# A decoder layer with 32 experts on one core: weights stored with index 4p+k instead of 128k+p

## The reference

```
h = rmsnorm(layernorm(x)) * norm_w                    # 1600 rows of 512
logits = h @ router_w.T ; top 4 of 32 experts per row, weights by softmax
gu = h_row @ w1[e]          # 512 x 512 : gate 256, up 256
ys = (silu(g) * u) @ w2[e]  # 256 x 512
out = x + sum over the 4 experts of weight * ys + (silu(h @ sg) * (h @ su)) @ sd
```

## Time and profile before

| what | value |
|---|---|
| median of 3 runs | 1313.39 us |
| the three runs | 1310.71, 1313.39, 1321.99 us |
| profiled execution | 1321.14 us, its span 1319.4 us |
| PE / PEld busy | 1189.7 / 933.1 us |
| DVE / ACT / POOL busy | 808.2 / 592.3 / 351.8 us |
| mean granted PE clock | 0.939 |

### The profile page before, as it was taken

The page is one execution under the profiler, slowest core; times in us unless marked ns, Lnnn a source line. Parts: engine busy times, 40 slices in busy tenths (PEclk is TensorE's granted clock), DMA queues, the critical chain, the costliest instruction groups (busy, mean ns, idle before and its releaser), DMA issues. The chain is left out here.

```text
span 1319.4 us, 20922 instructions
## 1 busy us (share of the span) xinstructions
PE 1189.7 (90%) x7761; PEld 933.1 (71%) x7762; DVE 808.2 (61%) x1392; ACT 592.3 (45%) x1402; POOL 351.8 (27%) x279
## 2 busy tenths in 40 slices
PE   7989999899989989989998989479989999999993
PEld 3457567667666756766676667278868999999892
DVE  1154686678678668667867865463226667676661
ACT  1134553454454445345435433241115666666661
POOL 0011102112202211210220121140222666666653
PEclk9888999889899988999989999589998999999997
DMA  7800000000000000000000000620256999999965
GB/s 270 246 36 2 1 9 9 13 8 8 13 10 6 14 13 8 8 13 8 8 14 13 8 9 14 189 81 26 64 217 192 270 293 276 294 274 278 261 132 63
DMA packets 70460, 121.10 MB, mean 92 GB/s; under 512 B 18503, under 2 KB 22135, under 8 KB 70251
## 3 DMA queue, kind: packets, MB, share of 16 engines
q1 hardware_dynamic: 52682, 82.46, 19.2%
q0 software_dynamic: 17728, 37.97, 13.4%
HBM read 93.55 MB, written 28.13 MB: 92 GB/s over the span
## 5 line engine op out<-in xcount | busy, mean ns | idle before, releaser
L1299 POOL TENSOR_TENSOR rall<-qkv_var,phalf 100x17 f32<-100x17 f32 x16 | 49.2, 3074 | 541.4 <-DVE qkv_var L1025 541.4
L375 PE MATMUL QS<-xh,wh 128*128 128x256 f32 x512 | 148.1, 289 | 0.0
L376 PE MATMUL QS<-xl,wh 128*128 128x256 f32 x512 | 145.5, 284 | 0.0
L377 PE MATMUL QS<-xh,wl 128*128 128x256 f32 x512 | 145.4, 284 | 0.0
L1365 POOL DMA_INDIRECT out_rows<-work,idx x64 | 110.6, 1728 | 120.6 <-issue 54.9
L375 PE MATMUL W<-wch,oth 128*100 128x512 f32 x256 | 115.2, 450 | 2.8 <-DVE otl L1093 2.8
L376 PE MATMUL W<-wcl,oth 128*100 128x512 f32 x256 | 111.3, 435 | 0.0
L377 PE MATMUL W<-wch,otl 128*100 128x512 f32 x256 | 109.5, 428 | 0.0
L376 PEld LDWEIGHTS QS<-xl,wh 128*128 128x128 f32 x512 | 99.0, 193 | 1.2
L375 PEld LDWEIGHTS QS<-xh,wh 128*128 128x128 f32 x512 | 98.8, 193 | 1.2
L377 PEld LDWEIGHTS QS<-xh,wl 128*128 128x128 f32 x512 | 98.8, 193 | 0.0
(11 more groups left out here) (204 smaller groups left out, 2882.2 us busy)
## 6 DMA issues: line engine op xcount, KB each, us to landing
raw<-in_w SPq DMA_DIRECT2D x24, 1024.0 KB
raw<-in_w SPq DMA_DIRECT2D x24, 512.0 KB
work<-in_w SPq DMA_DIRECT2D x8, 1024.0 KB
work<-in_w SPq DMA_DIRECT2D x8, 512.0 KB
hx_rows<-h3x SPq DMA_DIRECT2D x16, 212.5 KB
h_columns<-h3s SPq DMA_DIRECT2D x16, 200.0 KB
h3T<-h_columns SPq DMA_DIRECT2D x16, 200.0 KB, 4.7
out_rows<-ytiles POOLq DMA_DIRECT2D x16, 200.0 KB, 2.5
```

Of the source, the lines that this page charges most:

```text
L375: mm(dst, ah, bh, start=start, stop=False)
L376: mm(dst, ah, bl, start=False, stop=False)
L377: return mm(dst, al, bh, start=False, stop=stop)
L1299: return nc.gpsimd.tensor_tensor(out=dst, in0=src, in1=phalf[:, 0:src.shape[1]], op=ALU.pow)
```

## The change

Everything that is contracted over 512 is stored with index 4p+k: piece k on partition p holds row 4p+k. A weight matrix [512, n] is then one run of 4n numbers per partition. w1 comes in pieces of 8 KB instead of 2 KB, w2 (index 2p+k) in pieces of 4 KB, `sg` and `su` in pieces of 8 KB, the router in 512 bytes instead of 128. To match, DVE writes the 512 numbers of `h3x` in the order k, p (a step of 128 numbers between writes), reading in order. Since w2's rows are now 2p+v, the outputs of w1 must come in that order: of each 256 columns the even ones make tile 0 and the odd ones tile 1. The copy of w1's high part and the subtraction for its low part read every second number and write in order. `sd`, the attention weights and part 1 of the split (w2) keep their order. The gathers and scatters are as they were, in size and order.

```diff
+        cols = (slice(0, 2048), slice(2048, WX))
+        same = lambda w: w
+        order = ((lambda w: w.rearrange("p (m v q) -> p m v q", v=2, q=P), lambda w: w.rearrange("p (m q v) -> p m v q", v=2, q=P)),
+                 (same, same))
...
-                             a[n].rearrange("(k p) n -> p k n", p=P)).then_inc(s.ld_wx, 16)
+                             a[n].rearrange("(p k) n -> p k n" if n == "routerT" else "(k p) n -> p k n", p=P)).then_inc(s.ld_wx, 16)
...
-                                     a[n].rearrange("(k p) n -> p k n", p=P)).then_inc(s.ld_sh, 16)
+                                     a[n].rearrange("(k p) n -> p k n" if n == "sd" else "(p k) n -> p k n", p=P)).then_inc(s.ld_sh, 16)
...
-                src1 = a["w1"][bass.ds(e, 1), :, :].rearrange("e (k p) n -> p (e k) n", p=P)
-                src2 = a["w2"][bass.ds(e, 1), :, :].rearrange("e (k p) n -> p (e k) n", p=P)
-                return ((w1s[u].rearrange("p (k n) -> p k n", k=KC), src1),
-                        (w2s[u].rearrange("p (k n) -> p k n", k=FE // P), src2))
+                src1 = a["w1"][bass.ds(e, 1), :, :].rearrange("e (p k) n -> p (e k n)", p=P)
+                src2 = a["w2"][bass.ds(e, 1), :, :].rearrange("e (p k) n -> p (e k n)", p=P)
+                return ((w1s[u], src1), (w2s[u], src2))
...
-                c = (slice(0, 2048), slice(2048, WX))[part]
-                copy(wh[e % 2][:, c], slots_w[e % RING][:, c]).then_inc(m.wh, 1)
+                kept, drawn = order[part]
+                c = cols[part]
+                copy(kept(wh[e % 2][:, c]), drawn(slots_w[e % RING][:, c])).then_inc(m.wh, 1)
...
-                    nc.vector.scalar_tensor_tensor(out=h3x[:, 0:HID], in0=xc, scalar=rstd[2][:, 1:2], in1=normw[:, :],
+                    by_p = lambda v: v.rearrange("t (p k) -> t p k", k=KC)
+                    nc.vector.scalar_tensor_tensor(out=h3x[:, 0:HID].rearrange("t (k p) -> t p k", k=KC), in0=by_p(xc),
+                                                   scalar=rstd[2][:, 1:2], in1=by_p(normw[:, :]),
                                                    op0=ALU.mult, op1=ALU.mult).then_inc(s.ln3_h, 1)
...
-                c = (slice(0, 2048), slice(2048, WX))[part]
-                tt(wl[e % 2][:, c], slots_w[e % RING][:, c], wh[e % 2][:, c].bitcast(fp32), ALU.subtract).then_inc(m.wl, 1)
+                kept, drawn = order[part]
+                c = cols[part]
+                tt(kept(wl[e % 2][:, c]), drawn(slots_w[e % RING][:, c]), kept(wh[e % 2][:, c]).bitcast(fp32), ALU.subtract)\
+                    .then_inc(m.wl, 1)
```

More of the change, by code:

```diff
@@ L712, in _ @@
                                     for k in range(KC):
-                                        last = mm(QS[:, 1024 + P * f:1024 + P * (f + 1)], w1s[0][:, 512 * k + P * f:512 * k + P * (f + 1)],
+                                        c0 = 512 * k + FE * (f // 2)
+                                        last = mm(QS[:, 1024 + P * f:1024 + P * (f + 1)], w1s[0][:, c0 + f % 2:c0 + FE:2],
                                                   late_x[:, P * k:P * (k + 1)], start=k == 0, stop=k == KC - 1)
```

## The result

The changed kernel is slower: 1334.82 us median (1331.02 to 1343.68) against 1312.05 (1304.24 to 1321.99) in the same comparison, ratio 1.0179 with a 95% interval of 1.0093 to 1.0265. Built a second time among the experiments (e4_after) it gave 1.0141 [1.0108, 1.0174]. The forecast was 1317 us, 3.6 us over the median of 1313.39 that it started from, with 1331 as its upper end. So "slower" was right only by a hair, and the size and the range were wrong.

A forecast was written before the change was run, and what follows sets the result against it. PE was taken to bound the expert stage, with DMA engines nearly full; PE and DVE alternate in the decoder. Median 1313.39 + 4.8 (write of `h3x`) - 1 (weight loads) = 1317.2, predicted as 1317 us, range 1303 to 1331.

The forecast's parts named there:

- loads of expert weights: Expert stage, SP's queue: larger packets shorten the scatter chain's lag, -4.7 us (0 to -9.5) profiled, -1 us in a median run.
- write of `h3x`: Decoder steps, DVE: strided write takes 0.32 us longer, on the chain 15 times, +4.8 us (0 to 8.7).
- Rival B: Expert stage: POOL's scatter chain becomes the bound, its packets waiting behind 8 KB ones; 1340 us full case, chance 0.13.
- its case for a lag from half way on: Milder case of Rival B: late scatter periods begin half way through the experts, giving 1330 us.
- PE's clock: Closing caveat: the prediction is wrong if the clock of PE moves more than its terms; no size given.
- rule of 16-byte lines: SBUF page: fewer than two accesses per 16-byte line cost a penalty, so `h3x`'s write pays, 8-byte steps are free; no size.
- The splits of w1: ACT's copy and DVE's subtraction reading every second number: priced 0, 2.2 us of cover, upper end 12 us.
- Rival C: Splits of w1: strided reads are slow, 1329 us, or 1379 if every second number costs a slot; chance 0.06.
- The profiled execution against the median: Whole run: profiled 1321.14 us lies 7.75 above the median 1313.39, read as mostly scatter lag, leaving 1.75 in a median run.
- the 9.5 us of lag: Expert stage: late scatter chain costs the profiled execution 2.9 us at PE's weight loads plus 6.6 at the end.
- The burst, router, shared weights: Row stores before the experts (-3 to +3 us), router loads, and `sg` and `su` loads: each taken as 0.
- Rivals A and D: A: write free, DMA gain real, 1308.6 or 1306 us, chance 0.26. D: no penalty, no gain, 1313, chance 0.08.

The follow-up runs named there:

- e4_after: The changed kernel built once more, nothing altered, as base beside the other runs; ratio 1.0141 to the kernel before.
- f2_loads: The kernel before with only the expert weight loads changed, to 8 and 4 KB pieces in two DMAs (results not the reference's); ratio 1.0033.
- g4_no_w2: The changed kernel without the loads of w2 from the fifth expert on (results not the reference's); ratio 1.0076 to the kernel before.
- h1_strided: g1_four with DVE reading and writing in steps of 512 bytes when it makes `h3x`, values staying in place; ratio 1.0047 to the kernel before.
- g1_four: The kernel before with each expert's weights in four DMAs instead of two, pieces still 2 KB; ratio 0.9942.
- g3_rest_1kb: The changed kernel with expert weights in 1 KB pieces and four DMAs per expert; ratio 0.9996 to the kernel before.
- f4_1kb: The kernel before with expert weights in 1 KB pieces, four DMAs per expert, one for each half of the columns; ratio 0.9904.
- e3_split: The changed kernel with w2 in its old order in 2 KB pieces, so both splits of w1 read in order; ratio 1.013 to the kernel before.
- f1_before: The kernel before, unchanged, run and profiled again; ratio 1.000.
- f3_peread: The kernel before with router, `sg`, `su` in index 4p+k; DVE writes `h3x` in order and PE reads every fourth number; ratio 1.0011.
- g2_big4: The kernel before with 8 and 4 KB pieces in four DMAs, each to half of the partitions (results not the reference's); ratio 1.035.
- e2_write: The changed kernel with `h3x` written in order and its source read with a step of 16 bytes; ratio 1.0121 to the kernel before.

## Why the prediction was wrong

**The step that failed in its mechanism is the one on the loads of expert weights.** It read the engine time per byte, set the lower end of the gain at none because "time goes by bytes", and took -4.7 us of lag for the profiled execution and -1 us for a median run. The engine time did fall about as its upper end said (5.5% per KB). But the scatter chain does not pay by SP's bytes: it falls behind when a scatter of POOL takes more than 7.4 us to land, and with large pieces this comes sooner. A loss was excluded from the sum without a reason that bears on that, and left to a rival. In timed runs the loads alone cost 0.33% (f2_loads, +4.4 us, 1 to 8 by the interval), against -1 us forecast; in the changed kernel's profile the experts cost 9.0 us more. **The term that was mis-sized, and by more, is the write of `h3x`:** +4.8 us in the sum, 8.3 to 9.5 in the profiles, 12 to 14 between timed runs.

**Rival B held in its place and its releaser,** the landing of the scatter before, and its point of decision was near: a scatter and its wait against 9.37 us. The lag began a fifth of the way in (1080 us, of 1014 to 1321). Its mechanism, an 8 KB packet before each of POOL's packets, is not shown: before the lag, landings are no longer with 8 KB pieces (6.1 us) than with 2 KB (6.0). Its reason for a chance of only 0.13, "what a scatter loses it gets back after the burst", fell with g4_no_w2: the engines were busy 0.84 and 0.90, and the periods stayed at 9.83. Its price was too high: 23 us more for the full case, where 9.0 us more were lost in the profile and 4.4 between timed runs. That 1330, its case for a lag from half way on, came near the time (1334.8) was luck, because the write cost more than it had in the sum. On the page it drew on (the Trainium skill, DMA: Bandwidth & Descriptors, Queues, rings and completion order) an engine changes queues after a whole packet, and such a packet holds several descriptors. No run here shows single turns. That landings get longer with heavier loads (medians of 6.0, 7.1 and 9.1 us) agrees in direction.

**The write of `h3x`** was right in kind and mis-sized. Its own length was 0.32 forecast and 0.39 measured. The sum took 15 x 0.32 = 4.8 us with an end of 8.7; the profiles show 8.3 (changed kernel) and 9.5 (h1_strided), since it left out what the text named last as a danger, PE's clock. Between timed runs three pairs differ by it and little else: h1_strided - g1_four 1.05%, g3_rest_1kb - f4_1kb 0.92%, e4_after - f2_loads 1.08%, so 12 to 14 us with intervals of some 6 us each. The last two pairs hold the splits, the router and the shared weights as well. That the strided write is more than half of the whole loss is what all three pairs and f2_loads point to, and the interval of one pair alone would not prove it. Where the 3 to 5 us between the profiles' 9.5 and these 12 to 14 come from is open; they lie inside the intervals. The rule of 16-byte lines (the Trainium skill, SBUF — State Buffer, Specifications) was borne out in direction: steps of 16 and of 512 bytes cost the same. That every step of 8 bytes is free, as the prediction drew from it, holds for DVE's subtraction (2.29 us both times) and not for ACT's copy (1.90 to 2.06 us).

**The splits of w1** were priced at 0, and e3_split against e4_after says 0.1%, inside the intervals. ACT's copy did get 0.16 us longer, under the cover of 2.2. Rival C fell.

**The profiled execution against the median.** The inference that its 7.75 us over the median were lag was wrong: f1_before (1312.91 us) had a lag from 1142 us on and still was 8 us shorter, of which 7.4 lie before the first store. Start-up varies as much as the lag. The median of 1313.39 from three runs was low, too: 17 to 35 later runs of the same kernel have medians of 1317.7 to 1319.4. And the 9.5 us of lag counted 2.3 us too many: g1_four needs 290.4 us from first to last without lag, and the kernel before took 297.6, which is 7.2 more.

**The burst, router, shared weights** at 0: from the fourteenth store to the first scatter 211.2 us against 210.7, and f3_peread at 1.0011 agree. Rivals A and D fell with the write. (The first span is 207.5 to 212.2 us over all profiles, whatever the kernel, and g1_four has the shortest.)

The sum as measured: 4.4 us for the loads (f2_loads) and 12 to 14 for the rest make 16 to 19, against +3.8 forecast; e4_after is 0.0141 x 1318.5 = 18.6 us over.

**The better version** is f4_1kb: 1305.71 us median, 0.9904 of the kernel before, and 0.9904 / 1.0141 = 0.977 of the changed one. It goes the other way from the change. g1_four, with 2 KB pieces, is as good within the intervals.

## What to carry to other kernels

Before making the pieces of a bulk load larger, look at who shares the DMA engines with it: if a chain of small indirect DMAs beside it has little slack per period (here 9.37 us against a landing plus 1.93), the longest landings are what the load's shape is to be tuned for, and not its engine time. Here four DMAs instead of two helped, and pieces over 2 KB hurt. A lower end of "no loss" needs a reason on each chain that the resource serves, not on the transfer itself. And a few tenths of a microsecond before a PE that already idles 3 us per step cost twice: once as time, once as clock.

## What was not expected of the hardware

- Pieces of 512 bytes took 58 ns per KB of the engines' time (0.612 x 70 x 16 / 11.74), 1 KB pieces 48.3 (f4_1kb), 2 KB pieces 45.9, 8 and 4 KB pieces 43.4: little is won beyond 2 KB, and the fastest kernel is not the one with the least.
- A load into 64 partitions took 68 ns per KB, one into 128 43.4, with the same 8 and 4 KB pieces (g2_big4): 3.5% on the kernel.
- After the same wait of 3.25 us, 5 to 13 products ran at the low granted clock, in a pattern that repeats every four steps; after 3.63 us it was 10 to 12 in every step (g1_four, h1_strided).
- PE reads the source of a transpose with a step of 16 bytes in 362 ns instead of 340 (f3_peread), where DVE's row went from 0.75 to 1.17 us (e2_write).
- The kernel without lag has the busier DMA engines (1080 to 1250 us: g1_four 1.01, changed kernel 0.95), and the lag of g4_no_w2 began while they were busy 0.84.
- POOL's scatter instruction itself takes 1.60 us on average in kernels without lag (g1_four) and 1.96 to 2.11 with large pieces (changed kernel, g4_no_w2).
